# Self-attention units of a perceiver kernel: scores on 64 partitions, sums and values as TensorE products of both batches

## The reference

```
def attention_fwd(x, wq, wk, wv, wo, n_heads=32):
    ...
    xq = rotary_pos_emb(xq)
    xk = rotary_pos_emb(xk)
    scores = jnp.einsum('bqhd,bkhd->bhqk', xq, xk) * scale
    scores = jnp.where(causal[None, None], scores, NEG_INF)
    probs = jax.nn.softmax(scores.astype(jnp.float32), axis=-1).astype(xq.dtype)
    out = jnp.einsum('bhqk,bkhd->bqhd', probs, xv).reshape(B, T, C)
    return out @ wo.T
```

## Time and profile before

| | |
|---|---|
| three runs | 2836.49, 2840.89, 2844.17 us (median 2840.89) |
| profiled execution: its own time / its span | 2835.77 / 2834.0 us |
| PE busy | 2631.8 us, 93% |
| PEld busy | 2410.2 us, 85% |
| DVE busy | 1917.5 us, 68% |
| ACT busy | 1524.1 us, 54% |
| POOL busy | 1493.7 us, 53% |

### The profile page before, as it was taken

The page is one execution under the profiler, slowest core; times in us unless marked ns, Lnnn a source line. Parts: engine busy times, 40 slices in busy tenths (PEclk is TensorE's granted clock), DMA queues, the critical chain, the costliest instruction groups (busy, mean ns, idle before and its releaser), DMA issues. The chain is left out here.

```text
span 2834.0 us, 43610 instructions
## 1 busy us (share of the span) xinstructions
PE 2631.8 (93%) x17320; PEld 2410.2 (85%) x17320; DVE 1917.5 (68%) x2192; ACT 1524.1 (54%) x2702; POOL 1493.7 (53%) x1021
## 2 busy tenths in 40 slices
PE   7999999999999999999999999998867877997878
PEld 6899999999999999999999999997754445775667
DVE  2266776777667767766776677665559997786773
ACT  3455665566556656655665566554344442663552
POOL 2344754655555573574474475430029961794752
PEclk9999999999999999999999999999978998998879
DMA  5410110110111011011111010005230003331100
GB/s 202 135 46 23 61 48 29 54 54 31 34 58 39 25 52 61 23 54 46 38 47 54 23 61 25 29 34 191 73 125 30 1 15 119 127 131 46 49 1 15
DMA packets 90415, 163.81 MB, mean 58 GB/s; under 512 B 8114, under 2 KB 57522, under 8 KB 87658
## 3 DMA queue, kind: packets, MB, share of 16 engines
q1 hardware_dynamic: 81898, 152.70, 16.1%
q10 hardware_dynamic: 8320, 8.39, 0.9%
HBM read 143.17 MB, written 17.89 MB: 57 GB/s over the span
## 5 line engine op out<-in xcount | busy, mean ns | idle before, releaser
L357 POOL TENSOR_TENSOR xa_pt_lo<-xa_st,xa_pt_hi 128x1024 fp32r<-128x1024 f32 x255 | 510.3, 2035 | 596.1 <-ACT xa_pt_hi L543 596.1
L54 PE MATMUL xa_kv_ps<-ctx_wv_hi,ctx_hi 128*128 128x256 f32 (+1 forms) x1664 | 467.6, 281 | 3.1 <-DVE xa_v_lo L634 3.1
L56 PE MATMUL xa_kv_ps<-ctx_wv_hi,ctx_lo 128*128 128x256 f32 (+1 forms) x1664 | 469.7, 282 | 0.0
L55 PE MATMUL xa_kv_ps<-ctx_wv_lo,ctx_hi 128*128 128x256 f32 (+1 forms) x1664 | 465.4, 280 | 0.0
L54 PE MATMUL xa_kv_ps<-ctx_hi,ctx_wk_hi 128*128 128x402 f32 (+1 forms) x1024 | 356.4, 348 | 2.4 <-DVEq L711 2.2
L56 PE MATMUL xa_kv_ps<-ctx_hi,ctx_wk_lo 128*128 128x402 f32 (+1 forms) x1024 | 353.1, 345 | 0.0
L55 PE MATMUL xa_kv_ps<-ctx_lo,ctx_wk_hi 128*128 128x402 f32 (+1 forms) x1024 | 352.8, 344 | 0.0
L634 DVE TENSOR_TENSOR xa_v_lo<-xa_kv_ps,xa_v_hi 128x512 fp32r<-128x512 f32 (+1 forms) x224 | 146.2, 653 | 265.8 <-ACT xa_v_hi L516 264.7
L54 PEld LDWEIGHTS xa_kv_ps<-ctx_wv_hi,ctx_hi 128*128 128x128 f32 (+1 forms) x1664 | 306.4, 184 | 3.3 <-DVE xa_v_lo L634 3.3
L55 PEld LDWEIGHTS xa_kv_ps<-ctx_wv_lo,ctx_hi 128*128 128x128 f32 (+1 forms) x1664 | 308.5, 185 | 0.0
L56 PEld LDWEIGHTS xa_kv_ps<-ctx_wv_hi,ctx_lo 128*128 128x128 f32 (+1 forms) x1664 | 306.7, 184 | 0.0
(11 more groups left out here) (416 smaller groups left out, 7085.6 us busy)
## 6 DMA issues: line engine op xcount, KB each, us to landing
ca_nat<-in_ctx SPq DMA_DIRECT2D x48, 512.0 KB, 3.7
ctx_raw<-in_ctx_t SPq DMA_DIRECT2D x24, 804.0 KB, 6.7
ctx_wk_raw<-in_xa_wk SPq DMA_DIRECT2D x64, 256.0 KB, 2.8
ctx_wv_raw<-in_xa_wv SPq DMA_DIRECT2D x32, 512.0 KB, 4.4
q_raw<-in_xa_wq SPq DMA_DIRECT2D x8, 1024.0 KB, 4.9
q_scratch<-q_q_sb ACTq DMA_DIRECT2D x8, 1024.0 KB, 4.4
xa_q_raw<-q_scratch SPq DMA_DIRECT2D x64, 128.0 KB, 2.6
o_scratch<-xa_o_sb SPq DMA_DIRECT2D x64, 128.0 KB, 1.7
```

What stands on the lines that cost most here:

```text
L54: nc.tensor.matmul(out, left[0], right[0], start=first, stop=False)
L55: nc.tensor.matmul(out, left[0], right[1], start=False, stop=False)
L56: return nc.tensor.matmul(out, left[1], right[0], start=False, stop=last)
L357: nc.gpsimd.tensor_tensor(by_chunk(pt_lo, p), scored(j, p).rearrange("p g q c -> p g c q"), by_chunk(pt_hi, p).bitcast(F32), ALU.subtract) ...
```

## The change

The masked keys get half as many columns: a block has 4 heads (HA), and hm_half, the sum of the two halves of the head mask, serves both halves of the channels. A unit's scores become two products per batch, one over partitions 0 to 63 and one over 64 to 127, each with 256 columns into its own PSUM bank. GpSimd makes kb_hi and kb_lo. The exponentials are transposed without a division. In `values` the stationary operand is the whole pt (both batches, 128 columns), the moving one the values of both batches (2 x 32 columns); so each row also gets a result with the other batch's values, which isn't read. Two further matmuls per pair of heads against head_sum (128x2, ones for each head's keys) give the sums. VectorE takes their reciprocals from PSUM and multiplies the output by them, unit by unit. o_sb has the batches on 128 partitions, so sa3 transposes 128x128 pieces. Rounding wo is cut in four and moves into the loop; so does the fill of of_rest.

```diff
-o_sb = top.sb("o_sb", [L, B, H])
+o_sb = top.sb("o_sb", [P, RT, H])
...
+HA = HC // 2
...
-    kb_hi, kb_lo = (sc.sb(n, [P, 2, BR, HC, L], F32R) for n in ("kb_hi", "kb_lo"))
+    kb_hi, kb_lo = (sc.sb(n, [P, 2, BR, HA, L], F32R) for n in ("kb_hi", "kb_lo"))
+    hm_half, cm_half = sc.sb("hm_half", [P, HA]), sc.sb("cm_half", [P, HA, L])
...
+    nmx, rden = sc.sb("nmx", [P, 2, HC]), sc.sb("rden", [P, 2, HC])
+    head_sum = sc.sb("head_sum", [P, HP], F32R)
+    NO = 2
...
-    s_ps = sc.ps("s_ps", [P, 2, 512])
+    s_ps = sc.ps("s_ps", [P, 2, 2, 512])
...
-    o_ps = sc.ps("o_ps", [L, 2, BR, 512])
...
+    o_ps = sc.ps("o_ps", [P, NO, 512])
...
-    def blocks(eng, out, kt, n, sem):
...
+    def blocks(pool, out, kt, n):
...
-            end = eng.tensor_tensor(out[:, n % 2, b], kt[:, r, c, b * L:(b + 1) * L].bitcast(F32).unsqueeze(1)
-                                    .broadcast_to([P, HC, L]), wide(hm[:, :]), ALU.mult)
...
+            end = pool.tensor_tensor(out[:, n % 2, b], of_batches(kt, n)[:, b].unsqueeze(1)
+                                     .broadcast_to([P, HA, L]),
+                                     hm_half[:, :].unsqueeze(2).broadcast_to([P, HA, L]), ALU.mult)
...
-        blocks(nc.gpsimd, kb_hi, kt_hi, 0, kb_hi_set)
-        weights.zero(nc.gpsimd)
-        for n in range(NU + 1):
-            if n + 1 < NU:
...
-                blocks(nc.gpsimd, kb_hi, kt_hi, n + 1, kb_hi_set)
-            if n > 0:
-                m = n - 1
-                pool.wait_ge(r_set, m + 1)
-                nc.gpsimd.tensor_tensor(s_sb[:, m % NS], s_sb[:, m % NS], wide(rs_[:, m % 2, :]),
-                                        ALU.mult).then_inc(p_set, 1)
...
+        nc.gpsimd.tensor_tensor(hm_half[:, :], hm[:, 0:HA], hm[:, HA:HC], ALU.add).then_inc(half_set, 1)
+        nc.gpsimd.tensor_scalar(cm_half[:, :, :], cm[:, :].unsqueeze(1).broadcast_to([P, HA, L]), 1.0, 1.0,
+                                ALU.mult, ALU.mult).then_inc(half_set, 1)
+        pool.wait_ge(half_set, 1)
+        for n in range(NU):
+            if n >= 2:
+                pool.wait_ge(s_full, n - 1)
+            blocks(nc.gpsimd, kb_hi, kt_hi, n)
+            blocks(nc.gpsimd, kb_lo, kt_lo, n).then_inc(kb_set, 1)
+            if n == 0:
+                nc.gpsimd.memset(head_sum[:, :].bitcast(F32), 0.0).then_inc(sum_zero, 1)
+                pool.wait_ge(sum_zero, 1)
+                for h in range(HP):
+                    nc.gpsimd.memset(head_sum[h * L:(h + 1) * L, h:h + 1].bitcast(F32), 1.0).then_inc(sum_ones, 1)
+                pool.wait_ge(sum_ones, HP)
+            if n == 1:
+                weights.zero(nc.gpsimd)
...
-            pe.wait_ge(kb_hi_set, n + 1)
-            pe.wait_ge(kb_lo_set, n + 1)
+            pe.wait_ge(kb_set, n + 1)
...
-                end = product(nc, s_ps[:, n % 2, :], (qz_hi[:, r, c, b, :], qz_lo[:, r, c, b, :]),
-                              (kb_hi[:, n % 2, b].rearrange("p h l -> p (h l)"),
-                               kb_lo[:, n % 2, b].rearrange("p h l -> p (h l)")), b == 0, b == BR - 1)
+                for j in range(2):
+                    js = slice(j * HA * HD, (j + 1) * HA * HD)
+                    end = product(nc, s_ps[:, n % 2, j, 0:HA * L], (qz_hi[js, r, c, b, :], qz_lo[js, r, c, b, :]),
+                                  (kb_hi[js, n % 2, b].rearrange("p h l -> p (h l)"),
+                                   kb_lo[js, n % 2, b].rearrange("p h l -> p (h l)")), b == 0, b == BR - 1)
...
-            pe.wait_ge(p_set, n + 1)
+            pe.wait_ge(e_set, n + 1)
...
-            if c == 0 and r > 1:
-                pe.wait_ge(o_free, r - 1)
-            for b in range(BR):
-                for i in range(HC // HP):
-                    cs = slice(c * P + i * HP * HD, c * P + (i + 1) * HP * HD)
-                    ls = slice(b * L, (b + 1) * L)
-                    end = product(nc, o_ps[:, r % 2, b, cs], (pt_hi[:, n % 2, i, ls], pt_lo[:, n % 2, i, ls]),
-                                  (v_hi[:, r * BR + b, cs], v_lo[:, r * BR + b, cs]), True, True)
+            if n == 0:
+                pe.wait_ge(sum_ones, HP)
+            if n >= NO:
+                pe.wait_ge(o_free, n - NO + 1)
+            both = slice(r * BR, (r + 1) * BR)
+            out = o_ps[:, n % NO, 0:BR * P].rearrange("p (b d) -> p b d", b=BR)
+            for i in range(HC // HP):
+                os = slice(i * HP * HD, (i + 1) * HP * HD)
+                cs = slice(c * P + i * HP * HD, c * P + (i + 1) * HP * HD)
+                product(nc, out[:, :, os], (pt_hi[:, n % 2, i, :], pt_lo[:, n % 2, i, :]),
+                        (v_hi[:, both, cs], v_lo[:, both, cs]), True, True)
+                total = o_ps[:, n % NO, BR * P + i * HP:BR * P + (i + 1) * HP]
+                nc.tensor.matmul(total, pt_hi[:, n % 2, i, :], head_sum[:, :], start=True, stop=False)
+                end = nc.tensor.matmul(total, pt_lo[:, n % 2, i, :], head_sum[:, :], start=False, stop=True)
...
-        act.wait_ge(wo_in, 16)
-        nc.scalar.activation(wo_hi[:, :, :], wo_raw[:, :, :], ACT.Copy).then_inc(wo_hi_set, 1)
...
-                end = nc.scalar.activation(s, s, ACT.Exp, bias=nmx[:, n % 2, h:h + 1],
-                                           accum_out=sm[:, n % 2, h:h + 1])
+                end = nc.scalar.activation(s, s, ACT.Exp, bias=nmx[:, n % 2, h:h + 1])
...
+            if 3 <= n < 3 + KC:
+                act.wait_ge(wo_in, 16)
+                nc.scalar.activation(wo_hi[:, n - 3, :], wo_raw[:, n - 3, :], ACT.Copy).then_inc(wo_hi_set, 1)
...
-            s = s_sb[:, n % NS]
...
+            s = s_sb[:, n % NS].rearrange("p (j h) l -> p j (h l)", j=2)
...
-                out=s, in0=s_ps[:, n % 2, :].rearrange("p (h l) -> p h l", h=HC), scalar=SCALE,
-                in1=cm[:, :].unsqueeze(1).broadcast_to([P, HC, L]), op0=ALU.mult, op1=ALU.add)
+                out=s, in0=s_ps[:, n % 2, :, 0:HA * L], scalar=SCALE,
+                in1=cm_half[:, :, :].rearrange("p h l -> p (h l)").unsqueeze(1).broadcast_to([P, 2, HA * L]), op0=ALU.mult, op1=ALU.add)
...
-            nc.vector.tensor_reduce(nmx[:, n % 2, :], s, AX_X, ALU.max, negate=True).then_inc(d_set, 1)
...
-        def sums(n):
-            dve.wait_ge(e_set, n + 1)
-            nc.vector.reciprocal(rs_[:, n % 2, :], sm[:, n % 2, :]).then_inc(r_set, 1)
+            if n >= 2:
+                dve.wait_ge(e_set, n - 1)
+            nc.vector.tensor_reduce(nmx[:, n % 2, :], s_sb[:, n % NS], AX_X, ALU.max, negate=True).then_inc(d_set, 1)
...
-        def output(r):
-            dve.wait_ge(o_full, (r + 1) * KC)
-            nc.vector.tensor_copy(o_sb[:, r * BR:(r + 1) * BR, :], o_ps[:, r % 2]).then_inc(o_free, 1)
...
-        blocks(nc.vector, kb_lo, kt_lo, 0, kb_lo_set)
+        def output(n):
...
+            r, c = units[n]
+            dve.wait_ge(o_full, n + 1)
+            nc.vector.reciprocal(rden[:, n % 2, :], o_ps[:, n % NO, BR * P:BR * P + HC]).then_inc(rden_set, 1)
+            dve.wait_ge(rden_set, n + 1)
+            for b in range(BR):
+                ls = slice(b * L, (b + 1) * L)
+                end = nc.vector.tensor_tensor(
+                    o_sb[ls, r, c * P:(c + 1) * P].rearrange("p (h d) -> p h d", d=HD),
+                    o_ps[ls, n % NO, b * P:(b + 1) * P].rearrange("p (h d) -> p h d", d=HD),
+                    rden[ls, n % 2, :].unsqueeze(2).broadcast_to([L, HC, HD]), ALU.mult)
+            end.then_inc(o_free, 1)
...
-            if n + 1 < NU:
-                if n >= 1:
-                    dve.wait_ge(s_full, n)
-                blocks(nc.vector, kb_lo, kt_lo, n + 1, kb_lo_set)
...
-            if n > KC and n % KC == 2 % KC:
-                output(n // KC - 1)
-            if 1 <= n <= NU:
-                sums(n - 1)
...
-        output(RT - 1)
...
+            if n >= 3:
+                output(n - 3)
+        output(NU - 1)
...
-                for b in range(BR):
-                    o = k * P + b * L
-                    end = nc.tensor.transpose(t_ps[:, r, o:o + L], o_sb[:, r * BR + b, k * P:(k + 1) * P],
-                                              ident[0:L, 0:L])
+                ks = slice(k * P, (k + 1) * P)
+                end = nc.tensor.transpose(t_ps[:, r, ks], o_sb[:, r, ks], ident[:, :])
```

More of the change, by code:

```diff
@@ L2548, in _ @@
                     end.then_inc(v_free, 1)
-        o_sb = top.sb("o_sb", [L, B, H])
+        o_sb = top.sb("o_sb", [P, RT, H])
         weights.place(top)
         wo_hi, wo_lo = top.sb("wo_hi", [P, KC, H], F32R), top.sb("wo_lo", [P, KC, H], F32R)
+        HA = HC // 2
         with Scope(nc, "sa2") as sc:
-            kb_hi, kb_lo = (sc.sb(n, [P, 2, BR, HC, L], F32R) for n in ("kb_hi", "kb_lo"))
+            kb_hi, kb_lo = (sc.sb(n, [P, 2, BR, HA, L], F32R) for n in ("kb_hi", "kb_lo"))
+            hm_half, cm_half = sc.sb("hm_half", [P, HA]), sc.sb("cm_half", [P, HA, L])
             NS = 3
             s_sb = sc.sb("s_sb", [P, NS, HC, L])
```

(34 more changed lines are left out.)

12 lines of the change are left out of this document (5 added, 7 removed).

## The result

The changed kernel takes 2858.2 us (median of 6 runs, 2854.1 to 2863.0), the kernel before, on the same chip, 2838.3. The ratio is 1.0072, with a 95% interval from 1.0059 to 1.0086: slower by 20 us, where 40 were forecast.

What follows compares the result with a forecast made beforehand. TensorE at the low clock was taken as the bound: 7.95 us per unit against 5.93. Start 10.3, chain 121.7 and last output 1.1 gave a 133.1 us stage, +40, hence 2881 us; 8-in-10 range 2846 to 2892.

Steps and rivals of the forecast that it cites:

- start of 10.3 us: Stage start: GpSimd's helpers, three units of key blocks and fills before the scores of unit 2 can begin, 10.3 us.
- the scores, priced at 2.56 us at the low clock: TensorE's twelve score products of 256 columns cost as much as six of 512, 2.56 us per unit at low clock.
- the prediction's own sign for it: Sign of overlap in TensorE's scores: products of 256 columns under 0.2 us apart at the low clock would show the forecast wrong.
- the ring: Not forecast: chain of waits from one unit's scores through ScalarE and GpSimd to the next's; four units of 7.53 us.
- products on partitions 0 to 63 and 64 to 127 overlap where they meet: TensorE scores at low clock: three of twelve products vanish, 0.64 us per unit, 10 us in all, 2871; chance 0.12.
- the case that was held the likeliest: Low clock in nearly the whole stage, TensorE the chain, no overlap: 2881 us, range 2871 to 2890; chance 0.52.
- alternating clock: Rival: TensorE's clock alternates in the stage as before, half the chain at either level, about 2852 us; chance 0.18.
- cheap loads: Rival: TensorE loads cost by columns alone, twenty value and sum products at 0.107 us each, 2847 us; chance 0.03.
- Free changes of row count: Lower end of the likeliest case's range: TensorE's changes between 64-row and 128-row products cost nothing, 2871 us.
- The sum products: Eight new two-column products per unit on TensorE each cost a full load of 0.213 us: 1.70 us at low clock.
- The values: TensorE's 12 value products at 0.213 us take 2.56 us per unit, as the 24 before: no gain.
- Changes of row count: Two changes per unit between 64-row and 128-row products on TensorE, 0.21 us each at the low clock.

Runs made afterwards that it cites:

- the run per batch: Value products one per batch (24 of 64x32, not 12 of 128x64), against the changed kernel with sums by ScalarE and wo_lo one unit later (2826.0): 2826.7 us.

## Why the prediction was half right

**Right: direction, place and clock.** TensorE at the low clock is what the stage waits for, steady units are as long as its products, and the clock stays at 0.50 but for 3.4 us (2658.5 to 2661.9). VectorE, ScalarE and GpSimd gave back nothing in the steady units, as priced. The first four, where TensorE was not full, came 5.6 us closer together than before; the sum has that in its start of 10.3 us (measured: 9.2 from the first helper to the scores of unit 2).

**Wrong: the scores, priced at 2.56 us at the low clock, "no gain".** That is twelve steps of 0.213; they take six, 1.27 us less. This is the term that failed, and the prediction's own sign for it came true (score products of 256 columns less than 0.2 apart). Fourteen units at 1.27 are 17.8 of the 18.1 us by which the stage was priced too high (133.1 against 115.0, counted from the helpers on as in the forecast); what else was off, the ring among it, nearly cancels. It is measured by taking the overlap away: the unit is then 7.96 us (7.95 forecast), the stage 135.2 (133.1) and the time 2880.3 (2881). That the last pair is closer than the stage is luck: 2881 was counted from 2840.9 for the kernel before, which took 2838.0 beside this run. The rival "products on partitions 0 to 63 and 64 to 127 overlap where they meet" had the mechanism with a chance of 0.12 and the wrong size: I let only the products next to a change of group overlap, three of twelve, 0.64 us per unit. In fact whole runs of three overlap, 1.27 per unit. The sentence on which I chose, "no row here shows an overlap", was true and proved nothing, since no row of before had two row groups side by side. The term had no bound from below; half of its price, both groups side by side throughout, would have been one, and it is what was measured.

The measured 2858.2 lies inside 2846 to 2892, but not inside 2871 to 2890, the range of the case that was held the likeliest. The wide range reached so low for an alternating clock and for cheap loads, and neither came. (Free changes of row count alone would have given 2881 - 6.3 = 2874.7, not 2871.)

**Right in size.** The sum products: 1.70 forecast, 1.66 measured. The values: 24 x 0.107 and 12 x 0.213 cost the same, confirmed by the run per batch. The sum products start 0.21 apart, as those of the earlier trace rows. That speaks against the rule of the Trainium skill, TensorE: Matmul & The Clock Gate, section "LDWEIGHTS (loading the stationary operand)", which would have had 0.107. Changes of row count: 0.42 forecast per unit; in the unit shown the steps 2703.03 to 2703.31, 2703.31 to 2703.69 and 2704.54 to 2704.90 exceed 0.21 by 0.07, 0.17 and 0.15, together 0.39.

**Wrong, small: the moved rounding of wo.** The prediction has no term for it and so put it at nothing without a reason. Behind wo_lo's wait in GpSimd's queue stood the key blocks of the next unit; 3.1 us in the four units.

**Right, where the profile spoke against the easy view: the earlier trace rows.** 64-row products at the low clock with TensorE full were the only sign, from two stretches, and two pairs of runs with 64 and 128 rows bear them out for units in which TensorE is full. What a steady unit lost has thus two parts of about one size: 0.76 us more of TensorE's work at the low clock (6.69 against 5.93 of the earlier trace rows), and 1.08 (5.93 - 4.85) that the kernel before had from its stretches at the high one.

## What to carry to other kernels

Before splitting products into row groups, price both sides: on disjoint rows and banks (no run varied the banks) and issued within a few places of each other they took half the steps, but in place of 128-row products they can keep TensorE at the low clock, which cost more here than that gained. A product with two columns cost as much as one with 64 where the load set the pace, so sums that another engine reads out on its way are cheaper there. When a piece of work is moved into a loop, ask what is queued behind its wait.
